# A state-space image block: ffn index arithmetic for two image rows at once, softplus summed by TensorE, stages moved to other steps

## The reference, cut to what matters

```python
x = x + ss2d(ln_c(x))                # the state-space layer
t = to_tokens(x);  t = t + ffn(ln_t(t))

def ss2d(x):                          # D_INNER = 512, D_STATE = 16, L = 48*48 steps
    xh, z = split(x @ W_in)
    xc = depthwise_conv3x3(xh)        # over the image, SAME padding
    xp = xc @ W_xproj                 # 8 columns dt_r, 16 B, 16 C
    dt = softplus(dt_r @ W_dt + b_dt)
    dtN = dt @ W_dtN + b_dtN
    for t in range(L):                # one after another
        h = exp(dt_t * A) * h + (dtN_t * B_t) * x_t      # h: 8 x 512 x 16
        y_t = sum_n(h * C_t) + Dskip * x_t
    return (layernorm(y) * silu(z)) @ W_out + b_out

def ffn(v):                           # v: 256 values of a token
    hot = v > 0.5
    lo, hi, sa = first set index of hot[32:48], hot[40:56], hot[48:64]   # 0 if none
    val = lo + 16 * hi
    res = (val << sa) & 255 if hot[39], else val >> sa if hot[40], else 0
    amp = 2 where hot[0] and (hot[39] or hot[40]), else 0
    v[64:80] += amp * onehot(res & 15);  v[72:88] += amp * onehot(res >> 4)
    return v
```

## Time and profile before

| | |
|---|---|
| runs | 4034.44, 4012.58, 4027.85 us; median 4027.85 |
| profiled execution | 4022.24 us, its span 4020.4 us |
| DVE busy | 3622.2 us (90%), 12317 instructions |
| PE busy | 3251.8 us (81%) |
| POOL busy | 3133.2 us (78%) |
| ACT busy | 2944.1 us (73%) |
| DMA queue | 77.1% of 16 engines' span, 783.66 MB |

### The profile page before, as it was taken

One profiled execution on the slowest core, in us unless ns is written; L12 is line 12 of the kernel. 1 busy time (PEld: TensorE's weight loads), 2 busy tenths in 40 slices (PEclk: granted clock), 3 DMA queues, 4 the chain that ended last, 5 costly groups with the idle time before them and its releaser, 6 DMA issues.

```text
span 4020.4 us, 103342 instructions
## 1 busy us (share of the span) xinstructions
PE 3251.8 (81%) x33792; PEld 1589.3 (40%) x33792; DVE 3622.2 (90%) x12317; ACT 2944.1 (73%) x6050; POOL 3133.2 (78%) x5771
## 2 busy tenths in 40 slices
...
GB/s 67 219 202 203 213 191 206 190 208 205 208 196 214 199 211 196 215 194 205 197 216 199 207 196 213 199 205 193 206 201 199 201 203 209 202 206 205 192 192 80
DMA packets 383392, 790.26 MB, mean 197 GB/s; under 512 B 80517, under 2 KB 235142, under 8 KB 382854
## 3 DMA queue, kind: packets, MB, share of 16 engines
q1 hardware_dynamic: 382854, 783.66, 77.1%
...
## 4 chain that ended last, share of the span: by engine, by line
DVE 31%; PE 31%; ACT 26%; issue 7%; SPq 3%; POOL 2%; DMA 1%; ACTq 0%; POOLq 0%; DVEq 0%
ACT ps_a L638 8%; PE ps_s L583 6%; DVE h L885 6%; PE ps_y L492 6%; PE ps_s L528 4%; DVE ps_a L869 4%; DVE ps_a L872 4%; DVE h L888 4%; PE ps_s L537 3%; ACT ap L648 3%; PE ps_s L566 3%; PE ps_y L476 2%; ACT y L721 2%; DVE sz L941 2%; PE ps_s L584 2%
## 5 line engine op out<-in xcount | busy, mean ns | idle before, releaser
L638 ACT ACTIVATE ps_a<-dtb,a_n 128x384 f32<-128x384 f32 x2304 | 1253.6, 583 | 488.1 <-DVE h L888 472.3
L1169 POOL TENSOR_TENSOR h<-mp,up 128x128 f32<-128x128 f32 x2304 | 1052.5, 457 | 357.6 <-PE ps_y L492 147.4
L1159 POOL TENSOR_TENSOR mp<-ap,h 128x128 f32<-128x128 f32 x2304 | 1051.9, 457 | 358.1 <-ACT ap L648 242.7
L869 DVE TENSOR_TENSOR ps_a<-ps_a,h 128x192 f32<-128x192 f32 x2304 | 813.6, 353 | 239.6 <-ACT ps_a L638 236.7
L885 DVE SCALAR_TENSOR_TENSOR h<-xb,db,ps_a 128x192 f32<-128x192 f32 x2304 | 921.9, 400 | 24.0 <-PE ps_y L492 16.0
L888 DVE SCALAR_TENSOR_TENSOR h<-xb,db,ps_a 128x192 f32<-128x192 f32 x2304 | 927.2, 402 | 0.0
L492 PE MATMUL ps_y<-h,cw 64*32 64x256 f32 x18432 | 787.9, 461 | 71.9 <-DVE h L888 58.0
L872 DVE TENSOR_TENSOR ps_a<-ps_a,h 128x192 f32<-128x192 f32 x2304 | 807.7, 351 | 0.0
L648 ACT ACTIVATE ap<-dtb,a_n 128x256 f32<-128x256 f32 x1152 | 524.2, 509 | 251.1 <-DMA dtb<-xd 233.9
L1149 POOL TENSOR_TENSOR up<-xb,db 128x512 f32<-128x512 f32 x576 | 610.8, 1060 | 3.0 <-DMA xb<-xd 3.0
L492 PEld LDWEIGHTS ps_y<-h,cw 64*32 64x32 f32 x18432 | 315.7, 122 | 488.2 <-DVE h L888 244.6
...
## 6 DMA issues: line engine op xcount, KB each, us to landing
...
xin<-in_x_dram SPq DMA_DIRECT2D x144, 128.0 KB, 6.2
xd<-xtok SPq DMA_DIRECT2D x192, 96.0 KB
res<-in_x_dram SPq DMA_DIRECT2D x144, 128.0 KB, 5.4
out_dram<-res SPq DMA_DIRECT2D x144, 128.0 KB, 3.9
```

The costliest lines, as they stand in the source:

```text
L638: ins = act.activation(ps_a[buf][:, n, 0:2 * VD].rearrange("p (t d) -> p t d", t=2), dtb[:, u % DUNITS, 2 * buf:2 * buf + 2, 0:VD], ACT.Ex ...
L869: dve.tensor_tensor(a[:, 0], a[:, 0], last[:, 0], ALU.mult).then_inc(m0_done, 1)
L1159: pool.tensor_tensor(mp[:, G % 2], ap[:, Q % 2, G % 4], h[:, (G - 1) % HRING, :, VD:HALF], ALU.mult) \
L1169: pool.tensor_tensor(h[:, G % HRING, :, VD:HALF], mp[:, G % 2], up[:, Q % 2, G % 4], ALU.add) \
```

## The change

1. **ffn in pairs of rows.** `res`, `hot`, `score` and the small tiles hold six blocks of tokens. The ffn of rows 2p and 2p+1 is done at once, in 16 stages, mark, weigh and two adds: 36 instructions for a pair, in step 47 and in steps 0 to 9 of the next row, in every second row only. The comparison with 0.5 is folded into the operations that use it (`scalar_tensor_tensor` with `is_gt`), `found` is replaced by a bitwise and, mark and weigh are one instruction each. The logarithm and exponential of the second layernorm are done once for a pair; six DMAs store two rows.
2. **Softplus's sum by TensorE.** POOL's `finish_dt` is gone. relu(v) has a tile `rel` of its own; `transpose_dt` now is two accumulating matmuls per block (rel and dt against the identity), and `dtn_project` accumulates over rel and dt.
3. **Two halves of a row side by side.** `x_project`, `dt_project`, `dtn_project`, `xp`, `dbt` hold the first 24 columns of the row on partitions 0 to 63 and the others on 64 to 127; matmuls have 192 columns in place of 384 and alternate between the halves.
4. **One token buffer.** `dttok` is gone; dt in token order is copied into `xtok`, once x's stores have landed. `store_x` and `store_dt` go block by block. B and C bounce through DRAM in four DMAs in place of two.
5. **Positions.** One table `AT` gives every stage its distance in steps from its row's step 0. The weights are waited for one row earlier, and the loop has one more row at its end.

```diff
-SLOT = {
-    "conv": (0, 1, 3, 4), "xproj": (6,), "dtp": (8, 9, 11, 12), "xtok": (14, 15, 16), "yt": (18, 19, 20, 21),
-    "dttok": (23, 24, 26), "dtn": (27,), "out": (29, 30, 31), "z": (33, 34, 36, 37), "xlnT": (39, 40),
...
+AT = {
+    "conv": (-49, -47, -46, -45), "xproj": (-43,), "dtp": (-42, -42, -39, -39), "xtok": (-35, -34, -33),
...
+    "ffn": (95, 95, 96, 96, 97, 97, 98, 98, 99, 99, 100, 100, 101, 101, 102, 102, 103, 103, 104, 105),
...
             def copy_dttok(r, k):
                 act.wait_ge(dttok_done, r * KT + k + 1)
-                act.activation(dttok[:, k * DI:(k + 1) * DI], shared_bank("dttok", r, k)[:], ACT.Copy) \
+                if k == 0:
+                    act.wait_ge(x_stored, (r + 1) * 2 * len(X_PARTS) * SEM_DMA)
+                act.activation(xtok[:, k, :], shared_bank("dttok", r, k)[:], ACT.Copy) \
...
-            def dt_project(r, g):
+            def dt_project(r, pair):
...
+                banks = [take_bank("dtp", r, 2 * pair + half) for half in range(2)]
+                for n in range(2):
+                    g = 2 * pair + n
+                    for half in range(2):
+                        rows = slice(half * XP_ROWS, half * XP_ROWS + DTR + 1)
+                        mm = pe.matmul(banks[half][:, n * HTOK:(n + 1) * HTOK], wdt[rows, g * P:(g + 1) * P],
+                                       xp[rows].rearrange("p b w -> p w b"), start=n == 0, stop=n == 1,
...
                 for g in range(NG):
-                    mm = pe.transpose(bank[:, g * P:(g + 1) * P], dt[:, g, k * P:(k + 1) * P], ident[:])
+                    pe.matmul(bank[:, g * P:(g + 1) * P], rel[:, g, k * P:(k + 1) * P], ident[:], start=g == 0, stop=False,
+                              skip_group_check=True)
+                    mm = pe.matmul(bank[:, g * P:(g + 1) * P], dt[:, g, k * P:(k + 1) * P], ident[:], start=False,
+                                   stop=g == NG - 1, skip_group_check=True)
...
                 for g in range(NG):
-                    mm = pe.matmul(bank[0:B_ROW + NS, 0:TOK], wdtn[:, g, :], dt[:, g, :],
-                                   start=g == 0, stop=g == NG - 1)
+                    for part in (rel, dt):
+                        for half in range(2):
+                            lo = half * XP_ROWS
+                            mm = pe.matmul(bank[lo:lo + XP_ROWS, 0:HTOK], wdtn[:, g, :],
+                                           part[:, g, half * HTOK:(half + 1) * HTOK], start=g == 0 and part is rel,
...
-            def finish_dt(r, half):
-                pool.wait_ge(sp_log, r * 2 + half + 1)
-                part = dt[:, 2 * half:2 * half + 2, :].rearrange("p g t -> p (g t)")
-                pool.tensor_tensor(part, part, dttok[:, 2 * half * TOK:(2 * half + 2) * TOK], ALU.add).then_inc(dt_ready, 1)
...
+                for r, j in due("ffn", i, s):
+                    if r % 2 == 1 and j % 2 == place:
+                        ffn_part(r // 2, j)
```

More of the change, by code:

```diff
@@ new lines, in _ @@
+                    for r, j in due("exp", i, s):
+                        softplus_exp(r, j)
+                    for r, j in due("log", i, s):
+                        softplus_log(r, j)
+                    for r, j in due("dttok", i, s, COPY_LAG):
+                        copy_dttok(r, j)
+                    for r, j in due("copy_y", i, s):
+                        copy_y(r * KT + j)
+                    for r, j in due("y_log", i, s):
+                        y_log_var(r)
+                    for r, j in due("y_scale", i, s):
+                        y_scale(r)
```

604 lines of the change are left out of this document (294 added, 310 removed).

## The result

The changed kernel takes 3854.85 us (median of 4 runs) against 4024.05 us before (median of 4), a ratio of 0.9579 with a 95% interval of 0.9543 to 0.9614. The forecast was 3898 us. The profiled execution took 3861.87 us with a span of 3860.1.

A forecast was written before the change was run, and what follows sets the result against it. DVE's work was taken as the largest part (75.1 us a row, 5.5 idle), several bounds following one another. Work fell 2.7 us a row, idleness stayed 5.5: 48 x 2.7 = 130 us less, 3898 us, range 3780 to 4010.

The forecast's parts named there:

- ffn: DVE's ffn work: a pair of rows costs 5.7 us, a row 2.9 in place of 5.35, 2.5 us less.
- Steps 10 to 20: ACT's stretch: DVE idles 0.5 us in rows with ffn, 3 in others, mean 1.8, 1.2 us less.
- PE in the rows without ffn: DVE waits for PE at step 6, idling 3.5 us every second row, 1.7 us a row new.
- PE's amount: PE's work per row: transposes 4.3 us more, x_project 1.4 and dt_project 2.7 less, sum about 0.
- PE's halves do not overlap: Rival: PE's half-row matmuls run one after another, 7.1 us more PE work a row, 4170 us; chance 0.08.
- Step 32's wait: DVE's wait at step 32 for a dt load behind SP's stores of x goes: 1.1 us less.
- The one token buffer: ACT's copy of dt at step 23 waits for x's stores: 1.0 us new idleness, ends 0 and 3.
- Table loads: 46 more loads, at steps 40 and 42 of every second row, 1.28 us each, costing 0.35 us a row.
- Start: Before the first step and in the tail: taken as 0, ends -6 and +8 us in all.
- Rows of two lengths: Expected sign in the profile: rows of two lengths, the ones with ffn longer.
- Idleness moves and grows: Rival: token buffer wait, late PE and the exponentials' deficit add 3.3 us a row, 4055 us; chance 0.16.
- The moves take most idleness away: Rival: stores land in time, PE keeps its lead, idleness falls to 2.5 us a row, 3754 us; chance 0.14.

The follow-up runs named there:

- b_shift: The kernel before with two DVE instructions on 3 elements moved two steps (first layernorm's 19 to 21, y's 10 to 12); ratio 1.0001 to before.
- ffn_rows: reload38 with the ffn done for each row by itself again, in steps 47 to 9 of every row; ratio 0.9536 to the kernel before.
- reload38: The changed kernel with ACT's logarithm table loaded again at step 38 in place of 45, 46 loads less; ratio 0.9675 to the kernel before.
- b_ffn: The kernel before with its ffn at steps 47 to 7 in place of 40 to 0 and a finished row's store moved from step 6 to 12; ratio 0.9825.
- rows_later: ffn_rows with the dt stages one step later, make_db two steps later, B's and C's DRAM bounce at step 26; ratio 0.9506 to the kernel before.
- apart: The changed kernel with the halves' matmuls one half after the other in x_project, dt_project and dtn_project; ratio 0.9884 to the kernel before.
- dt_later: The changed kernel with the same move of the dt stages as rows_later and nothing else; ratio 0.9588 to the kernel before.
- pool_sum: The changed kernel with softplus's sum on POOL again, at steps 12 and 17, transposes and dtn_project reading dt alone; ratio 0.9698 to the kernel before.
- ffn40: ffn_rows with the ffn at steps 40 to 2, its logarithm and exponential at 39 and 40; ratio 1.0136 to the kernel before.
- act_back: ffn_rows with ACT's work of steps 8 to 16 and y's transposes at the steps of the kernel before; ratio 0.9781 to the kernel before.

## Why the prediction was right, and where it was not

- **The number** (3898 forecast, 3854.85 measured, range 3780 to 4010) and the sign were right, in part by luck. The sum was 2.7 us a row of work less and no more idleness; measured are 4.9 us of work less and 1.3 more idleness. The step that failed is "DVE's work is the largest part, and it counts nearly in full wherever it is removed, unless what then is late is ACT or PE", or rather its use: the exception stands in the sentence, but the sum takes the 2.7 in full. b_shift removes 59.6 us in ACT's stretch for nothing, and ffn_rows adds 87 us to reload38 and gains. The places of the ffn and of ACT's stages, which I had priced at about nothing, are worth 1.5 us a row (b_ffn) and more in the finished kernel.
- **ffn: 2.5 us a row less.** DVE's work fell by 4.9 us a row, not 2.7. The two shift instructions are 48.0 + 38.7 us in the kernel before and 16.8 + 18.2 after, 1.1 us a row (I had 0, ends 0.9 either way), make_db 0.2 as said, the rest, 3.6, I put down to the ffn. But the pair itself is not what pays: one row at a time in the same place is 1.4% faster than reload38, which differs in nothing but the pair, and as rows_later 0.7% faster than the changed kernel beside it (0.9506, at most 0.9532, against 0.9570, at least 0.9541).
- **Steps 10 to 20.** That ACT enters with its full lead after a long ffn and without it in the other rows came out in sign, at less than half the size. DVE idles 17.54 - 15.77 = 1.8 us there in the one row and 18.43 - 15.86 = 2.6 in the other, where I had 0.5 and 3. The mean, 2.2, is near my 1.8. In b_ffn the lead is worth about 0.75 us in this stretch.
- **PE in the rows without ffn: 3.5 us of idleness.** In steps 0 to 10 of such a row DVE idles 17.99 - 13.66 = 4.3 us, and waits at steps 4 and 8 (1.4 and 1.7 us in the mean), not at 6. About right, and it is the slack in which a row's ffn could stand. I counted it as a loss and didn't see that it argued against pairing.
- **PE's amount: about 0.** PE busy 3229.6, 3250 forecast, but two errors cancel. The halves overlap, as the conv let expect; the rival "PE's halves do not overlap" is refuted, and apart shows its direction. Counted from the traces, x_project takes 73.0 / 48 = 1.5 us a row (1.4 said), dtn_project 2.8 as said, the transposes of dt 4.6 more (4.3 said), but dt_project 204.9 / 48 = 4.3 (2.8 said); why it gains so little was not followed. Together that is 1.8 us a row more, not 0. Against it the matmuls that did not change take about 2.0 less, the sums over the states alone 0.9, at a mean granted clock of 0.888 where the profile before has 0.854. How much of that is the clock was not separated.
- **Step 32's wait** went, as said: 1.5 us in the mean row before, below 0.15 after. DVE's total for the exponentials did not: 238.3 after 236.7 us.
- **The one token buffer: 1.0 us.** ACT waits for SP's stores 75.9 us in all, 1.6 a row, within the 1 to 3 said. DVE's new waits at steps 24 and 26 are 0.9 and 1.4 us in the mean, and their price is about 0 by dt_later, which takes most of the second away and gains nothing.
- **Table loads.** Around one of the added loads (ACT in order of time):

```profile
2038.88 0.47 ACT L788 ACTIVATE xlnT<-ps_s 128x384 f32<-128x384 f32 x1
2039.37 1.28 ACT L674 ACT_TABLE_LOAD   x1
2040.66 1.09 ACT L674 ACTIVATE ps_a<-dtb,a_n 128x384 f32<-128x384 f32 x2
```

  1.29 us again, as in the earlier trace rows. By the Trainium skill, page "ScalarE: Activation LUTs", section "What ACT_TABLE_LOAD costs", a drain of 1.38 us should come on top; this trace shows none either, neither in front of the load (0.02 us) nor behind it. The loads do cost DVE 0.9 us at step 42 of every second row, 0.45 a row where 0.35 was said. Taking them away gained nothing, as reload38 shows.
- **Start: 0.** The first step is 10.4 us later. In front of it ACT's copy of dt waits for x's stores, and PE's transposes are twice as many. The second explains little: pool_sum, with half the transposes, starts its first step only 1.5 us earlier. The rest was not tested.
- **Rows of two lengths** came, but the other way round: the rows with a pair's ffn in steps 0 to 9 take 76.5 us and the others 77.9.
- **Rivals.** "Idleness moves and grows" was half true: +1.3 us a row, covered by more work saved than I had. "The moves take most idleness away" was not.

Of the 3.6 us a row, b_ffn shows 1.5 for the ffn's place alone, 0.45 of it where only the granted clock differs. In the finished kernel the places are worth more: ffn40 shows 5.4 for the ffn's, act_back 2.35 for ACT's and y's stages. These don't add, since each floor depends on the stretch before. pool_sum (0.65) and apart (2.0) price PE's parts. Pairing with its later table load costs 76.97 - 76.08 = 0.9.
